# Two of eight blocks of softmax probabilities turned by VectorE and DMA instead of TensorE

## The reference

```
x = x + LN(attention(LN(x)))
x = x + LN(ffn(LN(x)))

attention:  qkv = x @ w_qkv.T;  q, k, v = split(qkv)           # one head of width 256 does the work
            probs = softmax(q @ k.T / 4)                        # 1024 x 1024 for each batch element
            out = (probs @ v)  read as (256, 1024) and taken back as rows of 256
            out @ w_proj.T + b_proj
ffn:        16 experts, each takes its 1024 best tokens of 8192 (softmax gate, top k), gated GELU, scatter-add;
            and a shared expert over all tokens
```

## Time and profile before

| | us |
|---|---|
| median of three runs | 1951.45 |
| lowest and highest run | 1951.33, 1951.89 |
| the profiled execution | 1953.15 |
| its span | 1951.3 |
| attention stage | from 18.4 to about 566 |
| round 4, first logits to the next round's first product | 305.63 to 357.23 |

### The profile page before, as it was taken

The page is one execution under the profiler, slowest core; times in us unless marked ns, Lnnn a source line. Parts: engine busy times, 40 slices in busy tenths (PEclk is TensorE's granted clock), DMA queues, the critical chain, the costliest instruction groups (busy, mean ns, idle before and its releaser), DMA issues.

```text
span 1951.3 us, 29159 instructions
## 1 busy us (share of the span) xinstructions
PE 1924.1 (99%) x10638; PEld 1651.6 (85%) x10638; DVE 1369.1 (70%) x2618; ACT 1037.6 (53%) x1929; POOL 522.1 (27%) x626
## 2 busy tenths in 40 slices
PE   8999999999999999999999999999999999999996
PEld 6888888888888888888888888888888888888886
DVE  6777787777776788767777776756565756565647
ACT  5457576666655345445455554545454545455455
POOL 0031132123030000323432333243234323332146
PEclk9999999999999999999999999999999999999999
DMA  3103323324244111443434444444435344434566
GB/s 130 55 34 107 80 99 109 98 80 137 64 154 144 66 44 55 133 87 89 106 86 107 97 96 79 110 88 98 98 90 105 88 106 93 104 83 107 155 212 173
DMA packets 153339, 197.38 MB, mean 101 GB/s; under 512 B 104449, under 2 KB 121089, under 8 KB 145153
## 3 DMA queue, kind: packets, MB, share of 16 engines
q1 hardware_dynamic: 127824, 158.00, 25.8%
q0 software_dynamic: 25392, 37.77, 12.2%
HBM read 114.38 MB, written 59.34 MB: 89 GB/s over the span
## 4 chain that ended last, share of the span: by engine, by line
PE 67%; DVE 2%; ACT 0%; issue 0%; DVEq 0%; POOL 0%; ACTq 0%; POOLq 0%
PE mo_psD L1635 12%; PE mo_psG L60 8%; PE mo_psU L60 7%; PE mo_psG L61 7%; PE mo_psG L62 7%; PE mo_psU L62 7%; PE mo_psU L61 7%; PE mo_psD L1640 6%; PE mo_psD L60 1%; PE mo_psD L61 1%; PE mo_psD L62 1%; PE mo_psX L1356 1%; DVE mo_F L1957 0%; DVE mo_HF L1984 0%; DVE mo_junk_v L1939 0%
## 5 line engine op out<-in xcount | busy, mean ns | idle before, releaser
L1772 ACT ACTIVATE mo_HF<-mo_psG 128x512 f32<-128x512 f32 x320 | 191.8, 599 | 377.2 <-PE mo_psU L62 345.4
L2278 POOL DMA_INDIRECT ACC<-OUT,mo_GI x128 | 201.8, 1577 | 623.5 <-DVE OUT L2067 612.0
L1984 DVE TENSOR_TENSOR mo_HF<-mo_psU,mo_HF 128x512 f32<-128x512 f32 x320 | 220.1, 688 | 186.9 <-ACT mo_HF L1772 180.0
L1635 PE MATMUL mo_psD<-wd,mo_H_hi 128*128 128x512 f32 x1024 | 256.3, 392 | 0.3 <-DVE OUT L2067 0.3
L60 PE MATMUL mo_psG<-mo_XT_hi,wg_hi 128*128 128x512 f32 x640 | 253.7, 396 | 0.8 <-DVE mo_HF L1984 0.8
L60 PE MATMUL mo_psU<-mo_XT_hi,wu_hi 128*128 128x512 f32 x640 | 249.9, 391 | 0.0
L61 PE MATMUL mo_psG<-mo_XT_lo,wg_hi 128*128 128x512 f32 x640 | 249.8, 390 | 0.0
L62 PE MATMUL mo_psG<-mo_XT_hi,wg_lo 128*128 128x512 f32 x640 | 249.4, 390 | 0.0
L61 PE MATMUL mo_psU<-mo_XT_lo,wu_hi 128*128 128x512 f32 x640 | 249.1, 389 | 0.0
L62 PE MATMUL mo_psU<-mo_XT_hi,wu_lo 128*128 128x512 f32 x640 | 249.0, 389 | 0.0
L1635 PEld LDWEIGHTS mo_psD<-wd,mo_H_hi 128*128 128x128 f32 x1024 | 185.7, 188 | 35.2 <-DVE OUT L2067 0.5
(11 more groups left out here) (355 smaller groups left out, 3990.8 us busy)
## 6 DMA issues: line engine op xcount, KB each, us to landing
X1a<-wg_in SPq DMA_DIRECT2D x16, 1024.0 KB, 5.1
X1a<-wu_in SPq DMA_DIRECT2D x16, 1024.0 KB, 4.8
X1a<-wd_in SPq DMA_DIRECT2D x16, 1024.0 KB, 4.8
XN<-XG SPq DMA_DIRECT2D x8, 1088.0 KB, 4.2
X<-x_in SPq DMA_DIRECT2D x8, 1024.0 KB, 5.4
out_dram<-X SPq DMA_DIRECT2D x8, 1024.0 KB, 6.4
XN2T<-xn2T SPq DMA_DIRECT2D x8, 1024.0 KB, 5.1
X1a<-xt_in SPq DMA_DIRECT2D x7, 1024.0 KB
```

What stands on the lines that cost most here:

```text
L1635: pe.matmul(psD[:, t % 2, :], hidden(b, it)[0][:, t * P:(t + 1) * P], wd_both[:, it, :, :].rearrange("p z d -> p (z d)"), start=(it == 0), ...
L1772: a.activation(HF[:, it % 2, :], psG[:, it % 2, :], ACT.Gelu).then_inc(s_gelu, 1)
L1984: v.tensor_tensor(HF[:, it % 2, :], psU[:, it % 2, :], HF[:, it % 2, :], ALU.mult).then_inc(s_mul, 1)
L2278: g.indirect_dma_start(out=io["ACC"], out_offset=bass.IndirectOffsetOnAxis(ap=GI[n % 2][:, 4 * tb + t:4 * tb + t + 1], axis=0), in_=OUT[:, ...
```

## The change

Blocks 1 and 3 of each round are no longer turned by TensorE. VectorE turns them in 32x32 squares into `PW` (`blocks_of_p`), and SyncE then issues sixteen transfers (`exchange_p`), each of which takes one square column of one quadrant of 32 partitions to its place in another quadrant: 32 partitions x 8 runs of 32 values. They land in `PJ` for block 1, which is the memory of PT_lo, and in half of xn2T for block 3. ScalarE makes PT_hi from there in one instruction (`exchanged_p_hi`), VectorE PT_lo of block 1 and GpSimd that of block 3 (`exchanged_p_lo`). The order of the output products becomes 0, 2, 1, 4, 3, 5, 6, 7, in steps 2, 4, 5, 6, 7, 7, 8, 9. hi and lo of block 5 move from step 6's usual place behind that step's other work. `join` moves to steps 0, 1 and 2, and the store of XN behind the second exchange. Some semaphores of the setup are merged.

```diff
+        PJ = nc.alloc_sbuf_tensor_at("PJ", [P, 2, NT, P], F32, offset=nc.sbuf_base - 4 * 2 * S)
+        BY_DMA, BY_PE = (1, 3), (0, 2, 4, 5, 6, 7)
+        ORDER, OUT_STEP = (0, 2, 1, 4, 3, 5, 6, 7), (2, 4, 5, 6, 7, 7, 8, 9)
+        PW = c.XR0[:, :, :].rearrange("p k t -> p (k t)")
+        blocks = PW.rearrange("p (t k c) -> p t k c", k=4, c=32)
+        def landing(i):
+            return PJ[:, ORDER.index(i) % 2, :, :] if i == 1 else xn2T[:, 1, :].rearrange("p (t c) -> p t c", t=NT)
...
 SyncE
+            def exchange_p(r, i):
+                for a in range(4):
+                    for k in range(4):
+                        sp.dma_start(landing(i)[32 * k:32 * (k + 1), :, 32 * a:32 * (a + 1)],
+                                     blocks[32 * a:32 * (a + 1), :, k, :]).then_inc(s_pd, 16)
...
-                    wait(sp, s_sc, r - 1)
-                    sp.dma_start(rows_of(io["XN"], r - 2), ...
+                wait(sp, s_pv, 8 * r + ORDER.index(1) - 1)
+                wait(sp, s_pw, by_dma(r, 1) + 1)
+                exchange_p(r, 1)
+                if R.gate:
                     wait(sp, s_n2, r - 1)
                     sp.dma_start(io["XN2T"][r - 2], xn2T[:, :, :]).then_inc(s_xtst, 16)
 (load of xt, store of RS)
+                wait(sp, s_pw, by_dma(r, 3) + 1)
+                if R.gate:
+                    wait(sp, s_xtst, 16 * r - 16)
+                else:
+                    wait(sp, s_pl, r)
+                exchange_p(r, 3)
+                if R.gate:
+                    wait(sp, s_sc, r - 1)
+                    sp.dma_start(rows_of(io["XN"], r - 2), ...
 (load of rsb, output)
...
 TensorE
+                    if i1 in BY_PE:
                         wait(pe, s_exp, 8 * r + i1 + 1)
-                        wait(pe, s_ptl, 2 * (8 * r + i1))
+                        wait(pe, s_ptl, 2 * (7 * r + turned_in_front(i1)))
...
+                    for n in outputs_at(step):
+                        i2 = ORDER[n]
+                        wait(pe, s_os, 8 * r + n - 1)
+                        wait(pe, s_pth, 2 * (8 * r + n + 1))
 (eight matmuls of PT_hi)
+                        if i2 == 3:
+                            wait(pe, s_pl, r + 1)
+                        else:
+                            wait(pe, s_ptl, 2 * (7 * r + lo_in_front(n) + 1))
 (eight matmuls of PT_lo)
...
 ScalarE
+            def exchanged_p_hi(r, i):
+                n = ORDER.index(i)
+                wait(a, s_pv, 8 * r + n - 1)
+                wait(a, s_pd, 256 * (by_dma(r, i) + 1))
+                a.activation(PT[0][:, n % 2, :, :], landing(i), ACT.Copy).then_inc(s_pth, 2)
...
+                    if i1 in BY_PE and i1 != 5:
+                        turned_p_hi(r, i1)
 (the exponential of block i0)
-                    if R.gate and step in (2, 3):
-                        join(r, step - 2)
+                    if step == 4:
+                        exchanged_p_hi(r, 1)
+                    if step == 6:
+                        exchanged_p_hi(r, 3)
+                        turned_p_hi(r, 5)
+                    if R.gate and step < 3:
+                        join(r, (((0, 0),), ((1, 0),), ((0, 1), (1, 1)))[step])
...
 VectorE
+                    def exchanged_p_lo(i):
+                        n = ORDER.index(i)
+                        wait(v, s_pth, 2 * (8 * r + n + 1))
+                        v.tensor_tensor(PT[1][:, n % 2, :, :], landing(i), PT[0][:, n % 2, :, :].bitcast(F32),
+                                        ALU.subtract).then_inc(s_ptl, 2)
+                    def blocks_of_p(i):
+                        wait(v, s_pd, 256 * by_dma(r, i))
+                        wait(v, s_exp, 8 * r + i + 1)
+                        v.transpose(PW, Pr[:, i % 2, :]).then_inc(s_pw, 1)
+                    for n in outputs_at(step - 1):
+                        sum_output(n)
 (the maximum, O_lo of the same outputs, the reciprocal)
+                    if i1 in BY_PE and i1 != 5:
+                        turned_p_lo(i1)
+                    if step in (1, 4):
+                        blocks_of_p(BY_DMA[step // 4])
+                    if step == 4:
+                        exchanged_p_lo(1)
 (the tasks of the step)
+                    if step == 6:
+                        turned_p_lo(5)
...
 GpSimd
+            def exchanged_p_lo(r, i):
+                n = ORDER.index(i)
+                wait(g, s_pth, 2 * (8 * r + n + 1))
+                g.tensor_tensor(PT[1][:, n % 2, :, :], landing(i), PT[0][:, n % 2, :, :].bitcast(F32),
+                                ALU.subtract).then_inc(s_pl, 1)
...
                     deviation()
+                exchanged_p_lo(r, 3)
                 if R.post:
                     chain(2, r, s_r2)
```

More of the change, by code:

```diff
@@ L306, in logit_bank, with by_pe, by_dma, lo_in_front @@
             return 2 - 2 * (i % 2)
+        BY_DMA, BY_PE = (1, 3), (0, 2, 4, 5, 6, 7)
+        NQ, NE = len(BY_DMA), len(BY_PE)
+        ORDER, OUT_STEP = (0, 2, 1, 4, 3, 5, 6, 7), (2, 4, 5, 6, 7, 7, 8, 9)
[3 more added lines that the diff above has]
+            return PJ[:, ORDER.index(i) % 2, :, :] if i == 1 else xn2T[:, 1, :].rearrange("p (t c) -> p t c", t=NT)
+        def by_pe(r, i):
+            return NE * r + BY_PE.index(i)
+        def by_dma(r, i):
+            return NQ * r + BY_DMA.index(i)
+        def lo_in_front(n):
+            return sum(i != 3 for i in ORDER[:n])
+        def turned_in_front(i):
+            return lo_in_front(ORDER.index(BY_PE[BY_PE.index(i) - 1])) + 1 if i else 0
+        def outputs_at(step):
+            return [n for n in range(NT) if OUT_STEP[n] == step]
+        def read_tiles(r, i):
+            return (r, i - 2) if i >= 2 else (r - 1, NT + i - 2)
         class Round:
@@ L536, in body @@
                 for step in range(NT + 3):
[L537 to L539 removed]
+                    i0, i1 = step, step - 1
+                    for n in outputs_at(step - 1):
+                        i = ORDER[n]
+                        if n == 0:
                             wait(a, s_y, 4 * r)
[L541 to L550, removed]
+                        wait(a, s_ri, 8 * r + i + 1)
+                        wait(a, s_os, 8 * r + n + 1)
+                        a.activation(O[0][:, i, :], Osum[:, n % 2, :], ACT.Copy, scale=rinv[:, i:i + 1]).then_inc(s_oh, 1)
+                    if i1 in BY_PE and i1 != 5:
+                        turned_p_hi(r, i1)
                     if i0 < NT:
                         wait(a, s_max, 8 * r + i0 + 1)
[L553 removed]
+                        rp, ip = read_tiles(r, i0)
+                        if ip in BY_PE:
+                            wait(a, s_t, 2 * (by_pe(rp, ip) + 1))
+                        else:
+                            wait(a, s_pw, by_dma(rp, ip) + 1)
                         b = logit_bank(i0)
@@ L713, in body @@
                         scaled_lo(r + 1, (2, 3))
-                    if i3 >= 0:
-                        wait(v, s_oh, 8 * r + i3 + 1)
-                        v.scalar_tensor_tensor(O[1][:, i3, :], Osum[:, i3 % 2, :], rinv[:, i3:i3 + 1], O[0][:, i3, :].bitcast(F32),
-                                               ALU.mult, ALU.subtract).then_inc(s_ol, 1)
+                    for n in outputs_at(step - 1):
+                        output_lo(n)
                     if 0 <= i1 < NT:
```

90 lines of the change are left out of this document (50 added, 40 removed).

## The result

The kernel after takes 2030.77 us, median of four runs (2029.43 to 2031.8), against 1951.47 for the kernel before in runs beside it (1951.33 to 1951.89). The ratio is 1.0407, interval 1.0394 to 1.042: 79 us slower. The forecast was 1962.5, its range 1941 to 1984. The sign was right, the size was not.

What follows compares the result with a forecast made beforehand. TensorE, busy 99% of the span, was taken as the bound. Stalls on it against 1.58 us saved per round summed to +11 over eight rounds, from 1951.45 to 1962.5 us; range 1941 to 1984.

Steps and rivals of the forecast that it cites:

- TensorE's 12.6 us: Two of eight turns leave TensorE in eight rounds: 16 x 0.79 = 12.6 us, all on the path.
- VectorE's turn of 1.2 us: Each new VectorE instruction turning 128x1024 in 32x32 squares takes 1.2 us, with 0.6 and 2.4 as ends.
- The chain on ScalarE and VectorE: Round 4's sequence on both engines: maximum 2 at 318.4, exp 2 done 320.8, aggregation ended 327.75, maximum 6 done 341.1.
- The stall at turn 2: TensorE, ready to turn block 2 at 320.46 in round 4, waits about 0.35 us for exp 2.
- Issue: ... so 16 need some 7 us: On SyncE, 0.45 us from one issue to the next, so a block's 16 transfers need some 7 us.
- Landed 340.9 ... I take 343.1: Block 3's transfers behind RS land at 340.9 without its effect; signalled in order 343.1 to 344.7; 343.1 taken.
- Turn 6 at 346.0, stall 2.4: In round 4 TensorE wants turn 6 at 343.6 but gets it at 346.0, a stall of 2.4 us.
- TensorE's clock drops: Rival: TensorE's clock falls in the new gaps; stalls of 2 us in 64 called little, given nothing of its own.
- packets are slow: Rival, chance 0.10: at 55 ns per 128-byte packet, blocks 1 and 3 land late, about 8 us per round: 2026.
- the store of RS, 180 ns each: Upper end for packet price: RS's 64 writes of 4 bytes per engine take 11.5 us; 46 us per block.
- The cover holds: Rival, chance 0.34: transfers hide, VectorE keeps up, TensorE loses under 1.58 us per round: 1938.8, or 1944 with small stalls.
- VectorE's 9.6 us of gaps per round: Argument for "The cover holds": VectorE has 9.6 us of gaps per round against about 1.2 net added.

Runs made afterwards that it cites:

- experiment 9: The kernel of experiment 8 without its 16 transfers, so block 1 is not computed: 1950.81 us, ratio 0.9999 to the kernel before.
- experiment 3: The kernel after with RS stored in runs of 32 bytes instead of 4-byte values, transfers unchanged: 2006.1 us, ratio 1.0277 to the kernel before.
- experiment 5: The kernel after with 4 transfers per block instead of 16, each 128 partitions x 1 KB, RS unchanged, blocks landing unturned: 1968.3 us, ratio 1.009.
- experiment 1: The kernel after without its 32 exchange transfers and the waits for them, so blocks 1 and 3 are not computed: 1959.8 us, ratio 1.0037.
- experiment 8: The kernel of experiment 7 with hi 3 and lo 3 in front of hi 1 and lo 1: 1955.03 us, ratio 1.0018 to the kernel before.
- experiment 10: The kernel after, all transfers and RS kept, with hi, lo and output of block 5 in front of block 3's: 1979.56 us, ratio 1.0144.
- experiment 7: The kernel after with only block 1 turned by VectorE and transfers, block 3 turned by TensorE again: 1992.92 us, ratio 1.0215.

## Why the prediction was wrong, step by step

Times of the kernel after are given in the clock of the earlier trace rows (38.25 less).

- **TensorE's 12.6 us: right as work, not as time.** The page has 128 matmuls fewer (10510 for 10638), the 16 turns of eight. But also without any transfer TensorE's 6.3 us of one block don't arrive (experiment 9). The line total of the earlier trace rows did not confirm the price of 0.79: 66.7 us for 64 blocks is 1.04, the length of a record; 0.79 is from start to start.
- **VectorE's turn of 1.2 us: right.** The group of the new instruction, count, total and mean ns:

```profile
L799 DVE STREAM_TRANSPOSE XR<-Pr 128x1024 f32<-128x1024 f32 x16 | 19.9, 1246 | 18.5 <-DMA PJ<-XR 15.4 <-ACT Pr L615 3.1
```

- **The chain on ScalarE and VectorE: right.** Maximum 2 at 318.2 (forecast 318.4), exp 2 done at 320.8 (320.8), aggregation done at 327.4 (327.75), RS issued at 331.1 (331.6), maximum 6 done at 340.4 (341.1). The stall at turn 2 was 0.16, not 0.35. (The end of the round, 359.2 in the forecast, is 359.0 by its own terms; nothing hangs on it.)
- **"Issue: ... so 16 need some 7 us": the first step that failed.** I carried 0.45 over from stores and loads of HBM to a transfer from SBUF to SBUF, and gave it no range. It is 0.65, and 10.5 to 11.2 us for sixteen. At block 1 the error is small: landed at 329.8 instead of 327, which delays VectorE's turn of block 3 by 1.20 and costs TensorE nothing here. But XN2T is issued behind it, at 328.7, and block 3 waits for XN2T to land: its first issue comes 2.3 late (333.9 for 331.6), and its issues take 4 us more.
- **"Landed 340.9 ... I take 343.1": the second.** hi 3 began at 349.2. Of the 8.3 us over 340.9, 2.3 and 4.0 are those just named and 2.0 the time behind the last issue. I had treated RS as a limit on when signals arrive, and since its end (343.1) lay near my landing, it seemed to cost 2 us. With the data themselves held, a late start and the hold add up. Of the Trainium skill, "DMA: Bandwidth & Descriptors", section on queues, rings and completion order, I had used the rule that a semaphore increment lands only after every earlier write from that engine. No run speaks against it, but it gave me a bound where the windows of experiment 3 show a rate.
- **"Turn 6 at 346.0, stall 2.4": the place was right, and the releaser.** It came at 352.1, 8.83 late.
- **"TensorE's clock drops ... I give this nothing of its own": wrong, because the stalls were longer.** I had argued from stalls of 2 us. At 2.3 to 2.5 us that held in three rounds of four (experiment 5). Behind the waits of 4.25 to 11.07 us of the kernel after, turn and output take 5.0 to 6.5 us instead of 3.6, in all some 16 us that the sum lacked.
- **The rival "packets are slow" named 2026 us and was not what happened.** Its test was the packet's price:

```profile
DMA packets 3536, 0.43 MB, mean 47 GB/s; under 512 B 3536, under 2 KB 3536, under 8 KB 3536
q1 hardware_dynamic: 3536, 0.43, 29.1%
...
DMA packets 2014, 0.24 MB, mean 30 GB/s; under 512 B 2014, under 2 KB 2014, under 8 KB 2014
q1 hardware_dynamic: 2014, 0.24, 151.3%
```

  The first pair of lines is 357 to 366 us, block 1: 0.291 x 9 us x 16 engines / 3536 = 12 ns a packet, below the 16.7 that I had from the earlier trace rows (19.8 if its share of 118.2% is taken in as here). The second is 375 to 383, block 3 behind RS: 1.513 x 8 x 16 / 2014 = 96 ns. A packet is slow only in company. The rival's bound "the store of RS, 180 ns each" was the right row, read as a price of other transfers and not of what stands behind this one.
- **"The cover holds" (0.34) had too much weight.** Even without any transfer, experiments 1 and 9 gain nothing. Its argument, VectorE's 9.6 us of gaps per round, compares sums; what decides is order, and there only tenths of a microsecond are free: in experiment 9 one turn less is eaten at two places by 0.3 to 0.5 us each.

What stays open: how much of the loss another queue for half the issues would save (not tried), what the short runs cost where RS is quick, and why the packets behind RS are slow.

## What to carry to other kernels

Work that is taken off the bounding engine and spread over many small transfers is paid on the issuing queue: count issues first, at a price measured for that kind of transfer, and let the range hold twice the price of another kind. Then look at what is queued behind whatever waits for the landing, on every engine: experiments 8 and 10 won back 38 and 51 us by putting ready work in front of it, with the same transfers. Longer runs alone won 18, a quick RS alone 25; only fewer transfers won more, 63 (experiment 5, whose quadrants stay in place, so it is no complete kernel). And price the clock with every wait of some microseconds: it was a fifth of this loss. And ask what the DMA engines are doing when a transfer is issued: a store of 4-byte writes in front of it is not free.

## What the runs showed of the hardware that was not expected

- An issue of a small transfer from SBUF to SBUF took SyncE 0.60 to 0.65 us, with 32 or 256 packets and with 32 or 128 partitions; stores and loads of HBM beside it took 0.34 to 0.46, but a store right behind block 3's sixteen took 1.02 and the output 0.87.
- A store of 1024 values in 4-byte writes slowed the packets issued behind it from 12 to 96 ns, in the mean of 8 us. In 32-byte runs the same bytes did not.
- After 3.88 us (experiment 7) and 8.83 us (the kernel after) without work, round 4, TensorE had a granted clock of 0.50 and took 1.97 us for eight transposes that else take 1.03 to 1.09. After 1.14 us it had not dropped; after 2.3 to 2.5 us it had in one round of four (experiment 5).
- VectorE's turn in 32x32 squares of 128x1024 float32 takes 1.25 us, as long as a subtraction of that size.
- A subtraction with two SBUF inputs on VectorE took 3.02 us where GpSimd's addition had started 0.42 us before it (experiment 7), and 1.23 where it started 0.28 us before the addition, which then took 3.21 instead of 2.4 (the kernel after). "SBUF — State Buffer" of the Trainium skill calls the port pair that the two engines share an exclusive lock; both rows agree.
